# A six-layer attention stack and three sample stages on one core: other orders of the engines' work, a straight-line end, and a blended token shift

## The reference

```python
for i in range(6):                                  # 1: linear attention and a feed-forward part
    xn = layernorm(x, ln1_w[i], ln1_b[i])
    q, k, v = xn @ wq[i], xn @ wk[i], xn @ wv[i]    # 8 heads of 16
    q = softmax(q, axis=features of a head); k = softmax(k, axis=tokens)
    x = (q @ (k.T @ v)) @ wo[i] + bo[i] + x
    xn = layernorm(x, ln2_w[i], ln2_b[i])
    x = leaky_relu(xn @ w1[i]) @ w2[i] + x
# 2: spiking: y = relu(x @ W_fc.T)**2 @ W_proj.T; the spikes of 5 steps of a leaky sum, counted
# 3: state space: u = x @ Win.T + b; a convolution over time with a computed kernel (by Fourier
#    transforms); then y @ Wout.T + b
# 4: token shift and gate:
x_prev = x shifted by one token (zero first)
xr = mu_r * x + (1 - mu_r) * x_prev
xk = mu_k * x + (1 - mu_k) * x_prev
out = sigmoid(xr @ W_r.T) * (relu(xk @ W_k.T)**2 @ W_v.T)
```

## Time and profile before

| | |
|---|---|
| time, median of 3 runs | 846.43 us (846.15 to 846.81) |
| the profiled execution | 846.16 us, of which the instructions span 844.3 us |
| PE busy | 791.0 us, 94% of the span |
| DVE, ACT, POOL busy | 662.4, 584.7, 462.1 us |
| DMA | 13.7 MB, mean 16 GB/s |

### The profile page before, as it was taken

One profiled execution on the slowest core, in us unless ns is written; L12 is line 12 of the kernel. 1 busy time (PEld: TensorE's weight loads), 2 busy tenths in 40 slices (PEclk: granted clock), 3 DMA queues, 4 the chain that ended last, 5 costly groups with the idle time before them and its releaser, 6 DMA issues.

```text
span 844.3 us, 16194 instructions
## 1 busy us (share of the span) xinstructions
PE 791.0 (94%) x5354; PEld 687.8 (81%) x5354; DVE 662.4 (78%) x1937; ACT 584.7 (69%) x1244; POOL 462.1 (55%) x740
## 2 busy tenths in 40 slices
PE   7689999999999999999999999989999999998864
PEld 3468888999899989999899998878888887877752
DVE  4668788888788788788878787897875799999951
ACT  3466777787787777777777777778777657756353
POOL 6888556565576536544554445543454355566543
PEclk9799999999999999999999999999999999999996
DMA  9200000100000000100001000000000000000001
GB/s 258 94 0 2 1 1 1 39 1 2 1 26 14 2 2 1 38 2 1 1 2 39 1 1 1 1 1 3 1 1 1 2 1 2 2 14 26 14 14 38
DMA packets 19729, 13.70 MB, mean 16 GB/s; under 512 B 2488, under 2 KB 18495, under 8 KB 19647
## 3 DMA queue, kind: packets, MB, share of 16 engines
q1 hardware_dynamic: 19646, 12.67, 5.2%
HBM read 10.57 MB, written 2.10 MB: 15 GB/s over the span
## 4 chain that ended last, share of the span: by engine, by line
PE 76%; POOL 9%; DVE 7%; issue 4%; ACT 3%; DMA 0%; POOLq 0%; ACTq 0%; DVEq 0%
PE PS L317 68%; PE PS L327 8%; POOL XI L767 2%; ACT BIG L913 1%; POOL QB L877 1%; POOL RSTD L790 1%; POOL RSTD L797 1%; POOL RX L758 1%; ACT XR L956 1%; DVE QSM L1537 1%; DVE STATS L1273 1%; DVE STX L1258 1%; POOL R L725 1%; DVE ST L1194 0%; DVE XR L1315 0%
## 5 line engine op out<-in xcount | busy, mean ns | idle before, releaser
L317 PEld LDWEIGHTS PS<-W,HL 128*128 128x128 f32 x1536 | 194.1, 191 | 13.3 <-issue 5.3
L317 PE MATMUL PS<-W,HL 128*128 128x128 f32 x1536 | 202.0, 275 | 0.0
L969 ACT ACTIVATE HL<-PS 128x512 f32<-128x512 f32 x192 | 109.3, 593 | 14.5 <-PE PS L317 10.6
L779 POOL TENSOR_TENSOR JOIN<-STATS 128x8 f32<-128x8 f32 (+1 forms) x48 | 12.2, 254 | 159.0 <-DVE STATS L1273 159.0
L317 PE MATMUL PS<-X2H,W1L 128*128 128x512 f32 x192 | 91.6, 477 | 2.6 <-issue 2.2
L1138 ACT ACTIVATE EK<-PS,NKM 128x512 f32<-128x512 f32 x48 | 33.0, 688 | 76.7 <-DVE NKM L1498 76.7
L886 POOL TENSOR_TENSOR QB<-QB,QRC 128x512 f32<-128x512 f32 x48 | 50.9, 1061 | 56.5 <-DVE QRC L1540 56.5
L956 ACT ACTIVATE XR<-XI,RSTD 128x128 f32<-128x128 f32 x192 | 61.5, 393 | 25.4 <-POOL RSTD L797 25.3
L317 PE MATMUL PS<-X2H,W1H 128*128 128x512 f32 x192 | 76.2, 397 | 0.0
L317 PE MATMUL PS<-X2L,W1H 128*128 128x512 f32 x192 | 76.0, 396 | 0.0
L1273 DVE BATCH_NORM_STATS2 STATS<-XI 128x6 f32<-128x128 f32 x352 | 75.5, 277 | 0.1
(11 more groups left out here) (215 smaller groups left out, 2167.2 us busy)
## 6 DMA issues: line engine op xcount, KB each, us to landing
W<-in_w SPq DMA_DIRECT2D x12, 256.0 KB
X<-in_x SPq DMA_DIRECT2D x8, 256.0 KB, 4.6
out<-X SPq DMA_DIRECT2D x8, 256.0 KB, 2.3
QKV<-in_qkv SPq DMA_DIRECT2D x6, 192.0 KB, 2.8
FWD<-in_fwd SPq DMA_DIRECT2D x1, 1024.0 KB, 5.5
INV<-in_inv SPq DMA_DIRECT2D x1, 1024.0 KB, 8.1
WO<-in_wo SPq DMA_DIRECT2D x6, 64.0 KB
FWDX<-in_fwdx SPq DMA_DIRECT2D x1, 256.0 KB, 6.5
```

Of the source, the lines that this page charges most:

```text
L317: return nc.tensor.matmul(o, l, r, start=start, stop=stop, skip_group_check=True)
L969: nc.scalar.activation(HL[f][:, :], pH[f % 2][:, :], ACT.Prelu, alpha=LEAK).then_inc(s["hl"], 1)
```

## The change

It has four parts.

1. **Other orders in the layers.** Every engine's `step` is rewritten. On PE the step begins with `queries(n - 1)` (it stood in the middle, as the queries of item n) and ends with `hidden(n - 3, 3)`; read as a ring the order is nearly the one before, with `merge` later. On POOL the queries' two operations of item n-1 now open the step, `second_root` and `join` follow, then `first_root`, and `input_rstd(n + 3)`, `input_norm(n + 3)`, `first_low` and `centre_second` close it: read as a ring, they now stand between `join(n)` and the subtraction of item n. On DVE `input_stats(n + 3)` still closes the step, but the step now ends with the head maxima of item n, and `second_scale` (`XR2`) stands right ahead of them. At the first step of a layer PE's `output_bias` and DVE's `value_mask` stand behind the queries' sum and reciprocal.
2. **The state-space kernel earlier.** Three `kernel_slice` per step over 22 steps, and the spectrum in steps 37 to 39 instead of 48 and 49, in the bank pW.
3. **The end in straight calls.** Steps run only to n = 43; behind them each engine has a written list of calls (what is left of items 40 to 47, and every stage of the eight samples), each with the semaphores that its place needs. Results of a stage go to the sample's own part of XI where they went to one shared tile (X2S, XS, ZCNT, ZOUT, ZN, MEM), so the waits for that tile's reader are gone.
4. **The shift blended on DVE.** `key` and `gate` are one product each. ACT makes two scaled copies, DVE two blends. WK1, WK2, WR1 and WR2 are gone. WOUTT and BOUT are centred once, so `output_norm` needs no mean: two small POOL instructions per sample fewer.

The core of the diff:

```diff
@@ PE, the layers @@
+            def step(n, b, layer):
+                run(queries, n - 1)
+                if b == 0 and some(layer):
                     value_bias(layer)
+                run(second, n - 4, 1)
                 centre(n)
                 for unit in SPECTRUM.get(n, ()):
                     spectrum(unit)
+                run(weights_turn, n - 1)
+                run(second_turn, n - 3)
+                run(second, n - 4, 2)
+                run(context, n - 1)
+                run(second, n - 4, 3)
+                run(hidden, n - 3, 0)
+                run(values, n - 1)
+                if n == 1:
+                    output_bias(0)
+                if b == 0 and some(layer):
+                    output_bias(layer)
+                run(hidden, n - 3, 1)
+                if n in SLICES:
+                    kernel_slice(SLICES[n])
+                run(turn, n)
+                if n < 3:
+                    keep_busy(1)
+                run(merge, n - 1)
...
+                run(second, n - 3, 0)
+                run(hidden, n - 3, 2)
...
+                run(attend, n - 1)
+                run(keys, n)
+                run(hidden, n - 3, 3)
                 if n == 0:
+                    value_bias(0)
                     keep_busy(2)
@@ PE, the end (3 of its lines) @@
+            project_out(6, r_relu=4); transform(7, 0, back=7); transform(7, 1, back=7); key(4, o_sum=7)
...
+            gate(6, r_sig=6); key(6, rv=6); value(6, r_relu=7); shift_turn(7, blend=7); key(7, rv=7)
+            gate(7, r_sig=7); value(7, r_relu=8)
@@ PE, key and gate @@
-                mm(pY[:, :], WK1[:, :], SH[:, 1:1 + SEQ], True, False)
-                mm(pY[:, :], WK2[:, :], SH[:, 0:SEQ], False, True).then_inc(s["k2_ps"], 1)
+                mm(pY[:, :], WKT[:, :], XK[:, :]).then_inc(s["k2_ps"], 1)
...
-                    mm(pXT[:, j * P:(j + 1) * P], SH[:, 1 + j * P:1 + (j + 1) * P], WR1[:, :], True, False)
-                    last = mm(pXT[:, j * P:(j + 1) * P], SH[:, j * P:(j + 1) * P], WR2[:, :], False, True)
+                    last = mm(pXT[:, j * P:(j + 1) * P], XM[:, j * P:(j + 1) * P], WRT[:, :])
@@ POOL, the layers @@
+            def step(n, b, layer):
+                run(queries_shift, n - 1)
+                run(queries_scale, n - 1)
+                run(second_root, n - 2)
+                join(n)
+                run(first_root, n + 1)
+                if n + 1 in CHUNKS:
...
+                    exponents(CHUNKS[n + 1])
+                if 0 <= n < BATCH - 3:
+                    input_rstd(n + 3)
+                    input_norm(n + 3)
+                if b == 0:
+                    first_low(layer)
+                if b == 1:
+                    centre_second(layer)
@@ ACT, the part of the step that the next item waits for @@
+                run(context_copy, n - 1)
+                run(queries_exp, n - 1)
+                run(first_scale, n)
...
+                run(stream_copy, n)
...
+                run(keys_exp, n)
+                run(queries_copy, n)
+                run(rectified, n - 3, 3)
@@ DVE, the layers @@
+            def step(n, b, layer):
+                run(keys_reciprocal, n - 1)
+                run(first_stats, n + 1)
+                run(second_low, n - 3)
+                run(second_residual, n - 4)
+                run(queries_sum, n - 1)
+                run(queries_reciprocal, n - 1)
...
+                run(masked, n - 1)
+                run(scaled_merge, n - 1)
+                run(queries_out, n - 1)
+                run(stream_low, n)
+                run(first_residual, n - 1)
+                run(keys_max, n)
+                run(second_stats, n - 1)
...
+                run(second_scale, n - 2)
+                run(queries_blocks, n)
+                run(queries_max, n)
...
                 if n + 3 < BATCH:
                     input_stats(n + 3)
@@ DVE, the blend (new; ACT writes SHK and SHR, scaled by 1 - mu) @@
+            def blend(v):
...
+                stt(out=XK[:, :], in0=pX2[:, :], scalar=MU[:, 1:2], in1=SHK[:, 0:SEQ], op0=ALU.mult, op1=ALU.add)
+                stt(out=XM[:, :], in0=pX2[:, :], scalar=MU[:, 0:1], in1=SHR[:, 0:SEQ], op0=ALU.mult,
+                    op1=ALU.add).then_inc(s["blend"], 1)
@@ where the kernel's slices and its spectrum stand @@
-SLICES = {DECAY + 3 + i: 2 * i for i in range(PAIRS // 2)}
-KERNEL_OUT = DECAY + 3 + PAIRS // 2
+SLICES = {DECAY + 3 + i: 3 * i for i in range(1 + PAIRS // 3)}
+KERNEL_OUT = DECAY + 4 + PAIRS // 3
-SPECTRUM = {ITEMS: (0, 1, 2, 3), ITEMS + 1: (4, 5, 6, 7, 8)}
+SPECTRUM = {CENTRE + 4: (0, 1, 2, 3), CENTRE + 5: (4, 5, 6, 7), CENTRE + 6: (8,)}
```

More of the change, by code:

```diff
@@ L391, in kernel_slice @@
             def kernel_slice(i):
+                if i >= PAIRS:
+                    return
                 if i == 0:
@@ new lines, in _ @@
+            spiking_first(7, 2, relu=29); state_turn(5, blend=2); transform(4, 0, back=4); transform(4, 1, back=4)
+            value(0, o_sum=4); gate(1, cnt_z=7); spiking_first(7, 3, relu=30); spiking_second(7, 0, ym=7)
+            key(1, rv=1); project_in(5, r_sig=2); spiking_second(7, 1); spiking_second(7, 2); spiking_second(7, 3)
+            inverse(4); count(7, u_sum=6); shift_turn(2, st_T=6); project_out(4, r_relu=2); transform(5, 0, back=5)
+            transform(5, 1, back=5); state_turn(6, blend=3); value(1, o_sum=5); shift_turn(3, st_T=7)
@@ L769, in input_norm, with join_parts @@
                 last.then_inc(s["xi_init"], 1)
-            def join(first, end, turn):
+            def join_parts(first, end, turn):
                 def part(i):
```

990 lines of the change are left out of this document (476 added, 514 removed).

## The result

The changed kernel takes 922.49 us (median of 4 runs, 918.54 to 926.71), the kernel before 846.62 beside it: a ratio of 1.091, 95% interval 1.088 to 1.093. I had forecast 865, between 846 and 884. The sign was right; the loss is 76 us where I had 18. The profiled execution has a span of 920.5 us, against 844.3. One execution of a later kernel (experiment 9) ran at a mean granted clock of 0.649 and took 1126 us, and is left out.

The account below looks back on a forecast made before the run. PE was taken to bound the middle, the queries' loop the start, PE then DVE the end. Span 844.3 + 32.3 + 4.4 + 2 - 20.4 = 862.6, with time outside the span and the median's offset 865 us; range 846 to 884.

Parts of the forecast that it names:

- Start: First 120 us: the next input's work moves into the queries' loop; 32.3 us lost, between 23.5 and 41.
- Item 0: Start: item 0's subtraction comes near 28.4 us instead of 20.64, 7.8 us later.
- The four turns: Start, items 0 to 4: 4.1 us more per turn, 16.5 us; centring of W2 1.3 and slower clock 7.5 beside it.
- The turn to item 5: Start, item 4 to 5: no input any more, about 12.0 us against 12.83, minus 0.8 us.
- The clock's part: Start: PE's idle gaps lower its clock; 16 us in four turns if low throughout, half taken, 7.5 us.
- Middle: 120 to 540 us: PE full, nothing in an item's PE work changes; +2 us, between -2 and +6, spectrum's 4.4 beside it.
- the borders: Middle, five layer borders: PE's output_bias waits for value_mask, 0 to 1.2 us each; 3 us taken.
- The spectrum: Steps 37 to 39, where PE is full: the 18 products moved there take 4.4 us.
- End ahead: From 540 us to item 47's last residual: PE is the limit, 130 us against 141.4, gain 11.4 us.
- End behind: Behind item 47's last residual: DVE is the limit, 154 us against 162.9, gain 9 us.
- The rivals: End wins, 836 us, 9%; start free, 832, 5%; low clock at start and end idle as before, 890, 10%; even, 3%.
- The signs: Profile after: subtractions every 17 to 21 us up to item 4, later steps 11.9 us, last residual near 708, blends 0.7 us.

Follow-up runs that it names:

- experiment 9: experiment 5 with POOL's second root of item n-2 taken ahead of the input's work: 854.28 us, ratio 1.007 to the kernel before.
- experiment 1: The changed kernel with the inputs' root and normalisation (POOL) and statistics (DVE) moved back out of the queries' loop: 898.65 us, ratio 1.061.
- experiment 8: The kernel before with only the input's statistics, root and norm and the exponents moved ahead of the subtraction: 891.82 us, ratio 1.052.
- experiment 2: The changed kernel with only POOL's 16 exponents instructions moved behind the queries' scaling: 906.05 us, ratio 1.070.
- experiment 3: The changed kernel with W1's low part and W2's centring behind the scaling one step later, value mask ahead of DVE's sum and reciprocal: 896.39 us, ratio 1.059.
- experiment 12: experiment 11 with the bias, mask and weight preparation of each layer one item later, as in the kernel before: 851.45 us, ratio 1.0063.
- experiment 5: The changed kernel with inputs, exponents, layers' weights and value mask moved out of the loop and the spectrum one step later: 856.94 us, ratio 1.013.
- experiment 11: experiment 5 with the loop's order of POOL, DVE and PE taken from the kernel before; blend and written-out end stay: 852.36 us, ratio 1.0056.
- experiment 10: experiment 5 with the loop's order of POOL and DVE taken from the kernel before; blend and written-out end stay: 873.55 us, ratio 1.031.

## Why the prediction was right in sign and wrong in size

- **Start, +32.3 forecast, +38.0 measured.** The mechanism holds, and experiments 1 and 8 show it from both sides. Item 0 came 7.6 us later (28.21 against 20.64), forecast 7.8. The four turns cost 29.4 us, forecast 16.5 + 1.3 + 7.5 = 25.3. The turn to item 5 was to gain 0.8 and lost 1.0. The first turn, 22.06 us, has the value mask in its chain as well (PE waited 10.7 us for it), which I had looked for at the later borders only. The clock's part was a half of a bound, and a rough one (half of 16 is 8, and I wrote 7.5); in the turns the four transposes take 1.09 us and not 0.63, and the products on the chain behind them 4.84 and 5.26 us in two turns, against 3.87 in the middle: 0.5 and 1.0 to 1.4 us, together 1.4 to 1.9 us a turn (24 matmuls there, 28 in the middle's piece, so it is rather more), and my 1.9 was about right. By the rule of the Trainium skill ("TensorE: Matmul & The Clock Gate", section "Why this matters for your kernels") I had put the full 4 us a turn beside it; the granted clock over the four turns was 0.73, 0.84, 0.82 and 0.83, between its two levels of 1.2 and 2.4 GHz, so the trace agrees with that rule in kind and not with its full price.
- **Middle, +6.4 forecast, +52.3 measured: the step that failed.** I wrote "Nothing in an item's PE work changes" and priced the borders at "between 0 and 1.2 us each". The first sentence is true of the work and didn't matter. I had followed the loop of the queries through the inputs and stopped there: that loop runs through all 48 items, and any POOL instruction between `first_root` and the subtraction is in it. Two sorts that I had seen in the same list stood there: sixteen `exponents` (experiment 2: 15.8 us) and, at five borders, W1's low part and W2's centring (with the mask, experiment 3: 24.0 us). I even counted W1's low part and the centring once, at item 0 and in item 1's turn, as terms of the start, and did not carry them to the five later borders. I looked at the mask instead, and PE waited 2.5 us for it after item 0. And I put the clock at nothing there: it fell six times behind waits of PE, which is some 10 us of the 52.3. The assumption behind it was that "in the middle the loop of the queries has slack". Before, a step was 11.88 us and PE was full, so the loop's own length could not be seen; it was under 11.88 us by an amount that I never worked out. With PE's work fitting in 12.25 us and a loop of 13.20 there was none. Experiments 8 and 2 bound it: one instruction of 1.0 us makes the step of the kernel before 1.01 us longer, so it had next to no slack.
- **The spectrum, +4.4.** Right in kind, too small. The steps from item 34 to 39, in which the coefficients, DVE's butterflies and the spectrum's products stand, are 10.0 us longer than before in the changed kernel (two stretches at the lower clock included, 3.2 us) and 7.6 in experiment 12; I had counted PE's products only. In one step PE waited 2.1 us for a butterfly, and the step took 17.26 us; with the spectrum one step later (experiment 5) that step took 11.62 and the one two behind it 13.87 in place of 12.54. The rest is argued from their place, not tried alone.
- **End ahead, -11.4 forecast, -12.6 measured.** Right, PE-limited as I had it, and the same in all runs with the written-out end.
- **End behind, -9 forecast, -1.6 measured.** A sum with its parts right but one: DVE's work 133.2 (133.4), gaps 6.8 (7), idle at the very end 21.3 (13.5). I had taken 14 us of DVE's work as lying beside the last chain of 27.5 us; if the chain is as long as that estimate, about 6 did. The blend's price was right (0.74 us for 0.69), and so was that it is no free gain: it was worth 4.8 us here and cost 9 in the old order.
- **The rivals.** None of them was a loss in the middle. The signs did hold the number that gives it away, steps of 11.9 us (12.4 with three slices) from 120 us on, where 13.20 came; but I named it as a mark of being right and didn't ask what a longer step would mean. The range's upper end of 884 came from the start's clock and the end, and left the middle +6 at most.

What stays open: which instruction holds the border steps of experiments 11 and 12 one us above those of before, how POOL's pieces and the mask share experiment 3's gain, and whether and where experiment 9 gains.

## What to carry to other kernels

- A loop that closes over several engines has a length of its own, and a full engine hides it. Work it out before judging an order: from one execution of an instruction to its next, what must stand between. Then ask of every instruction in the new list, of all stages and not only of the one looked at, whether it stands inside it. A 1 us instruction of the idlest engine cost 1 us in each step here.
- An order for one engine has no worth by itself: POOL's and DVE's old ones beside PE's and ACT's new ones took 873.6 us (experiment 10), all new ones 856.9 (experiment 5), and the old ones of all but ACT 852.4 (experiment 11).
- Taking work off a full engine onto another gains only where the other has room at that place: the same blend was worth 4.8 us or cost 9.
- A wait of the matrix engine can be paid for twice. Before you put a longer step down to an instruction in it, read its granted clock: here 3.4 us at the lower level made a step 1.6 us longer with no other change.

## What the runs showed of the hardware

The same instructions of POOL and DVE took different times by what ran beside them. POOL's subtraction took 1.06 us in most steps and 1.51 in 16 of 48 (in one before), and its mean rose from 1078 to 1215 ns with the new order. The timeline of both engines at item 13 shows how:

```profile
232.60 1.04 POOL L689 TENSOR_TENSOR BIG<-LA,IOTA 128x512 f32<-128x512 f32 x1
...
233.09 1.10 DVE L1321 TENSOR_TENSOR X2L<-X2F,X2H 128x512 fp32r<-128x512 f32 x1 [0.38 <-ACT X2F L925]
...
233.60 1.51 POOL L763 TENSOR_TENSOR QB<-QB,QMX 128x512 f32<-128x512 f32 x1
234.24 0.69 DVE L1365 TENSOR_TENSOR XI<-PS,XI 128x512 f32<-128x512 f32 x1
```

X2L's subtraction (two operands in SBUF) starts while POOL works on L689 and takes 1.10 us; POOL's next instruction then takes 1.51. Without a two-operand instruction beside them they take 0.69 and 1.06. XI's sum, which reads PSUM and SBUF, is at its usual 0.69 us beside the same POOL instruction. W1's low part took 1.74 us beside X2L at the border step shown above and 1.26 to 1.27 in the five others; before it was 1.27 once and 1.72 to 1.74 five times. DVE's L1418, with two operands in SBUF, averaged 1.08 us before: 0.99 to 1.67 in the five cases in which POOL was within a 128x512 sum as it began, 0.69 in the three others; the same instruction is 0.66 to 0.69 in the new end, where none of its eight begins beside such a sum. In the loop this is up to 0.45 us a step on the chain. The Trainium skill ("SBUF — State Buffer", section "SBUF: two separate sides") says that the port pair which the two engines share is held for a whole instruction, by a VectorE instruction with two SBUF inputs too, and that the other engine waits. The trace agrees: X2L's extra 0.41 us is most of the 0.55 that were left of L689 when it began, and the subtraction's extra 0.45 most of the 0.59 that were then left of X2L. Experiment 2 took L689 away from that place: the subtraction is at 1.06 us there (the row at 227.81 above), and X2L, which now begins half-way through the subtraction, takes 1.11.

The blends, with one operand in PSUM, took 0.74 us each, and so are priced by the row of that kind and not by the 1.08.
